# Loads of a streamed weight moved from the sync engine's list to the scalar engine's program

## What is computed

```
e    = 50 gathered table rows of 300 numbers for each batch row
h    = concat(attn_pool(e, w1..), attn_pool(e, w3..)) @ w5 + b5        # 300 wide
f7   = (h[:, iu] * h[:, ju] * g) @ w7 + b7      # all 44850 pairs i<j, w7 is 44850 x 300
out8 = concat(h @ w6 + b6, f7) @ w8 + b8
z    = einsum('bu,bku->bk', out8, label_embedding)   # 200 label rows of 300 for each batch row
y    = top MLP(concat(z, dense_ctx))
```

## Time and profile before

| | |
|---|---|
| runs | 2052.7, 2054.82, 2057.39 us; median 2054.82 |
| profiled execution | span 1864.9 us from the first to the last instruction; the page gives no device time of its own, and the median lies 189.9 us above the span |
| PE busy | 1703.9 us, 91% of the span |
| DVE busy | 1676.7 us, 90% |
| ACT busy | 1036.3 us, 56% |
| moved by DMA | 563.23 MB, mean 302 GB/s |
| SP's queue (q1) | 499.93 MB, 70.2% of the 16 engines' span |
| POOL's queue (q0) | 61.64 MB, 10.6% |

### The profile page before, as it was taken

The page is one execution under the profiler, slowest core; times in us unless marked ns, Lnnn a source line. Parts: engine busy times, 40 slices in busy tenths (PEclk is TensorE's granted clock), DMA queues, the critical chain, the costliest instruction groups (busy, mean ns, idle before and its releaser), DMA issues.

```text
span 1864.9 us, 26157 instructions
## 1 busy us (share of the span) xinstructions
PE 1703.9 (91%) x7132; PEld 1255.0 (67%) x7132; DVE 1676.7 (90%) x5836; ACT 1036.3 (56%) x3238; POOL 558.9 (30%) x413
## 2 busy tenths in 40 slices
PE   2788999999999999999999999999998999998841
PEld 1555667777777777777777677777776777775531
DVE  5898979989999889999999999899997888967785
ACT  3776684684466644466654675455753545454534
POOL 7774706828300134400078018500000000000053
PEclk8889999999999999999999999999999999999975
DMA  8378966757988689989768766998749999989985
GB/s 276 105 259 300 331 216 189 240 169 268 383 322 301 240 327 350 352 330 343 286 232 322 271 256 207 380 370 335 254 149 379 418 379 366 406 337 419 419 352 243
DMA packets 97949, 563.23 MB, mean 302 GB/s; under 512 B 16591, under 2 KB 16837, under 8 KB 72205
## 3 DMA queue, kind: packets, MB, share of 16 engines
q1 hardware_dynamic: 78525, 499.93, 70.2%
q0 software_dynamic: 19264, 61.64, 10.6%
q10 hardware_dynamic: 16, 0.00, 0.0%
HBM read 561.51 MB, written 0.00 MB: 301 GB/s over the span
## 4 chain that ended last, share of the span: by engine, by line
PE 54%; DVE 25%; DMA 11%; issue 4%; POOL 4%; ACT 3%; SPq 0%; DVEq 0%; ACTq 0%; POOLq 0%
PE acc L956 45%; DVE junk L580 11%; DVE qa L622 8%; DMA w_sb<-in_w 7%; DVE prod L734 6%; DMA lab<-in_labels 3%; POOL x L526 3%; PE coarse L807 2%; PE acc L872 1%; PE misc L879 1%; ACT heads L1067 1%; PE acc L941 1%; PE acc L854 1%; PE acc L857 1%; PE coarse L941 1%
## 5 line engine op out<-in xcount | busy, mean ns | idle before, releaser
L956 PE MATMUL acc<-w_sb,prod 128*128 128x300 f32 (+2 forms) x5680 | 1537.7, 421 | 52.9 <-DMA w_sb<-in_w 34.7
L956 PEld LDWEIGHTS acc<-w_sb,prod 128*128 128x128 f32 (+2 forms) x5680 | 1047.2, 192 | 402.8 <-DMA w_sb<-in_w 45.1
L1169 ACT ACTIVATE prod<-prod,g_all 128x256 f32<-128x256 f32 (+3 forms) x1625 | 690.7, 470 | 487.1 <-DVE prod L734 484.9
L526 POOL DMA_INDIRECT x<-in_tbl,ids_sb x376 | 485.8, 1292 | 672.5 <-DVE qa L622 565.2
L734 DVE TENSOR_TENSOR prod<-fine,coarse 128x1280 f32<-128x1280 f32 (+4 forms) x325 | 424.3, 1310 | 92.2 <-PE coarse L807 89.8
L580 DVE SCALAR_TENSOR_TENSOR junk<-lab,out 128x300 f32<-128x300 f32 x1056 | 424.6, 463 | 21.0 <-DMA lab<-in_labels 20.7
L580 DVE SCALAR_TENSOR_TENSOR junk<-x,score_u 128x300 f32<-128x300 f32 x752 | 303.6, 465 | 20.3 <-DMA x<-in_tbl,ids_sb 20.2
L622 DVE SCALAR_TENSOR_TENSOR qa<-x,ex,qa 128x300 f32<-128x300 f32 x628 | 282.6, 519 | 0.0
L557 POOL TENSOR_TENSOR x<-x,out 128x2400 f32<-128x2400 f32 x6 | 31.6, 5264 | 602.2 <-ACT out L1042 593.3
L1067 ACT ACTIVATE heads<-x 128x300 f32<-128x300 f32 x376 | 152.2, 405 | 25.8 <-DMA x<-in_tbl,ids_sb 24.8
L580 DVE SCALAR_TENSOR_TENSOR junk<-x,out 128x300 f32<-128x300 f32 x344 | 137.6, 463 | 0.0
(11 more groups left out here) (112 smaller groups left out, 628.0 us busy)
## 6 DMA issues: line engine op xcount, KB each, us to landing
w_sb<-in_w SPq DMA_DIRECT2D x325, 750.0 KB, 6.5
lab<-in_labels SPq DMA_DIRECT2D x140, 1200.0 KB, 7.8
x<-in_labels SPq DMA_DIRECT2D x60, 1200.0 KB, 8.7
x<-in_tbl,ids_sb POOLq DMA_INDIRECT x376, 5.5
prod<-in_v_i SPq DMA_DIRECT2D x1, 710.0 KB, 4.3
prod<-in_v_j SPq DMA_DIRECT2D x1, 710.0 KB, 7.3
w_sb<-in_w SPq DMA_DIRECT2D x1, 703.1 KB
top_sb<-in_top SPq DMA_DIRECT2D x1, 512.0 KB
```

Source lines behind the costliest of these rows:

```text
L526: pool.indirect_dma_start(out=row_of(t, n), out_offset=None, in_=tables[n], in_offset=bass.IndirectOffsetOnAxis(ap=ids_sb[:, t, n:n + 1], ...
L956: last = pe.matmul(acc[:, t % 3, 0:EMB], prod[0:rows, u % RING, m, t % 2 * P:(t % 2 + 1) * P], w7_sb[0:rows, u % W7_RING, m * EMB:(m + 1) ...
L1169: act.activation(chunk, chunk, ACT.Copy, scale=g_all[0:rows, pair:pair + 1]).then_inc(chunk_ready, 1)
```

## The change

SP issues only the first four loads of w7 and then the label slabs. The other 321 loads of w7 are issued by ACT, each right after it has scaled the last chunk of unit u, for unit u + 2. The condition on PE is the one of before (PE has finished unit n - 4, which is u - 2); new is that ACT must have finished scaling unit u, and that the transfers run on ACT's queue, which so far carried eight stores of 512 bytes.

```diff
             for kind, n in LOADS:
                 if kind == "w7":
-                    if n >= W7_RING:
-                        sp.wait_ge(unit_used, n - W7_RING + 1)
-                    sp.dma_start(w7_sb[:, n % W7_RING, :], w7[n % UNITS]).then_inc(w7_loaded[n % W7_RING], 16)
+                    if n < W7_RING:
+                        sp.dma_start(w7_sb[:, n, :], w7[n]).then_inc(w7_loaded[n], 16)
                     continue
...
+            def load_w7(n):
+
+                act.wait_ge(unit_used, n - W7_RING + 1)
+                act.dma_start(w7_sb[:, n % W7_RING, :], w7[n % UNITS]).then_inc(w7_loaded[n % W7_RING], 16)
+
...
                     if m == 1 and u + RING < TOTAL:
                         pick_window(u + RING)
+                    if m == FINE - 1 and W7_RING <= u + 2 < TOTAL:
+                        load_w7(u + 2)
```

## The result

The changed kernel took 2066.11 us (median of 7 runs, 2060.07 to 2069.23), the kernel before 2055.2 us beside it (7 runs, 2051.5 to 2058.04). The ratio is 1.0047, with a 95% interval of 1.0035 to 1.0059. That is a small loss of 9.7 us (7.2 to 12.1), against 6.6 us in the forecast.

What follows compares the result with a forecast made beforehand. Loads of w7 were late behind slabs in one queue, and DMA was the bound from 1660 us. Terms: -1.5 + 0 + 2.0 + 3.6 + 2.5 = 6.6 us slower, median 2054.8 to 2061.4 us, range 2046 to 2075.

Steps and rivals of the forecast that it cites:

- Sign and size: Whole kernel: slower by 6.6 us, the median going from 2054.8 to 2061.4 us; chance 0.42.
- Issue and wait on ACT, 0: ACT's program: 321 issues are covered by its waiting, and the new wait holds back nothing that could run; 0 us.
- A queue of its own: Loads of w7 beside a slab backlog: w7 gets 38% of 423 GB/s and lands in 6.9 us, including 2.1 us latency.
- The stall at 236 us: Load of unit 37: 4.1 us gained, 2.6 lost to three earlier slabs in the single-tile stage; net gain 1.5 us.
- The stalls at 1037 and 1205 us: Unit 180's load gains at most 3.9 us, offset by slabs: 0; at 1205 w7 passes a slab: 2.0 us lost.
- The stall at 1427 us: Before unit 248: PE's stall becomes a wait for the cross; two more loads pass the slab, 3.6 us lost.
- The end: From 1660 us, DMA-bound: later w7 issue and slabs not needed yet taking the rate lose 2.5 us.
- Later issue elsewhere: Loads also wait for the scaling two units ahead; unit 26's lead of 4.66 us just enough; 0, bounds 0 and 3.
- Waits of DVE for slabs above 23.8 us: Changed profile, whole span: DVE would wait for slabs more than 23.8 us in all.

Runs made afterwards that it cites:

- before again: Also called e1: the kernel before, unchanged, timed and profiled once more; 2048.78 us against 2047.65, ratio 1.0006, profiled span 2043.2 us.
- e5_after_two_slabs_first: The changed kernel with two label slabs moved in SP's list ahead of the burst of six slabs for `x`; ratio to the kernel before 0.9972.
- e10_end_act_slabs_held: The kernel before with ACT issuing the last 39 loads of w7, SP still waiting where it used to issue them; ratio 1.0044.
- e11_end_late_issue_sync: The kernel before, SP's loads of w7 for units 286 to 324 also waiting for the scaled chunks two units ahead; ratio 1.0034.

## Why the prediction was right, and where it was not

**Sign and size: right.** +6.6 us forecast, +9.7 (7.2 to 12.1) measured.

**Issue and wait on ACT, 0: right.** The wait alone gave 0.9999. The issues cost nothing either where nothing else changed: units 207 to 246 took 220.3 to 220.6 us and units 250 to 289 took 210.1 us, whether ACT issued their loads or SP.

**A queue of its own: the share was right, the latency too small.** The views give no landing times of loads on ACT's queue, but they count the packets of each queue. From 1600.2 to 1613.8 us after, when both streams had work waiting (packets, MB, share of the engines' time; q1 is SP's queue and q10 ACT's):

```profile
q1 hardware_dynamic: 425, 3.62, 62.9%
q10 hardware_dynamic: 390, 2.15, 38.1%
```

So w7 moved 2.15 of 5.77 MB, 37%, where I had assumed 38%. The times of its packets in the trace give the landings: the loads of units 247, 248 and 249 ended 8.4 to 8.7 us after their issue, not 6.9. Their bytes took 4.7 to 5.0 us, against the 4.8 of my sum; the first packet moved only 3.5 to 3.7 us after the issue, where I had put 2.1.

The slabs beside them say the same, by the landing of the first and of the fourth of the burst of six. After, issued at 1595.0 and 1596.3:

```profile
DMA to landing us min/median/max: 5.2/5.2/5.2
...
DMA to landing us min/median/max: 17.5/17.5/17.5
```

They landed 13.6 us apart, 4.5 us for each slab. All six of before again, issued from 1582.9 to 1585.6:

```profile
DMA to landing us min/median/max: 5.5/11.6/17.4
```

That is 14.6 us for five, 2.9 each. Slabs thus ran at 2.9 / 4.5 = 64% of the rate beside w7, where I had assumed 62%.

**The stall at 236 us, gain 1.5: the size may be luck.** The first slabs went out from 274 to 293 us, not at 320. Units 5 to 50 took 179.9 to 183.2 us in the six kernels with before's handling of them, mean 182.2, and 177.7 to 181.6, mean 180.1, in the five with after's: a gain of 2.1, less than single executions differ by. The stall that was to go wasn't there. In before again the load of unit 37 was as late as in the first profile (issued at 322.7, landed at 338.4 by its packets), but PE stood in unit 36 at that time, for nothing that the profile shows, and reached unit 37 at 345.6:

```profile
339.24 2.37 PE L956 MATMUL acc<-w_sb,prod 126*128 126x300 f32 x4 [6.10 <-issue]
```

The loss that was to come did: after, PE waited 3.7 us for w7 before units 22, 23 and 25, beside the slabs, against 2.6 in my sum. What gives the rest back isn't shown.

**The stalls at 1037 and 1205 us, 0 and a loss of 2.0: neither was there.** Both lie just behind places where the executions from e1 on had the erratic waits of DVE (units 176 and 205), which may have given the slabs time. Before again had no slab wait there either, and units 178 to 204 and 207 to 246 took the same in all. The step that failed is taking single stalls of one profiled execution for stalls of the timed runs. In their place stands one that I had not priced: DVE waited 1.64 us for a slab at 937.23, and units 118 to 175 took 0.3 to 3.7 us longer in every kernel in which ACT issues w7 there. (The gathers that I took to have a third of the rate near 1037 moved 2.17 of 8.08 MB, a quarter.)

**The stall at 1427 us, loss 3.6: right in mechanism.** DVE's wait was to be 13 to 14 us and was 13.62, 3.2 us more. PE lost 4.5 us from unit 246 to 250. `e5_after_two_slabs_first` shows the cause by taking it away.

**The end, loss 2.5: the term was mis-sized, and half of its reason was wrong.** It measured 5.8 us. I had given two reasons: loads issued later at the start of the stage, and slabs running ahead of need. `e10_end_act_slabs_held` takes the second away and loses as much; `e11_end_late_issue_sync` adds the first alone, with a longer delay, and loses 7 us. The lateness was bigger than I took it, because the load stands behind other work of ACT. And I had held that where DMA is the bound bytes are only handed on: the stretch ran at 403, 404 and 411 GB/s with the loads issued late (after and the two runs just named), with a DMA share of 1.00, and at 418 GB/s in before again. The bytes did not go to the other stream; fewer of them moved in the time. In `e11_end_late_issue_sync` the engines ran short of work; after, the slower slices have shares of 0.97 and more, and why less moved in them isn't shown.

**Later issue elsewhere, 0: right within the bound of 3 us, for a wrong reason in part.** I had the load go out when ACT has scaled the last chunk, which gave a lead of 4.66 us for unit 26, just enough. After, that lead was 8.5 us, since ACT issues ahead of its scaling (last section). Between units 5 and 36 the load went out a median of 7.7 us ahead of its use after and 8.9 in before again, and units 5 to 50 took no longer. A wait for the scaling itself, on SP's list, left 6.2 us there and cost 30 us in all.

**Waits of DVE for slabs above 23.8 us: wrong as a number,** 18.2, since the 23.8 belong to the other kind of execution; against 13.1 they rose.

## What to carry to other kernels

Splitting a queue changes two things at once: which bytes pass which, and what each issue waits behind in its new program. Price each at the place where the stream is tight, since both hide where it isn't. A stream that gets its own queue takes rate from the other, so the order within the other queue has to be set anew; here the move lost 0.5% alone and gained 0.3% with two slabs moved up. Where transfers are the bound, issue them as soon as their places fall free, from an engine that waits for nothing else.

## What the runs showed of the hardware

A profiled execution can lack waits that the timed ones have: 1864.9 us and 2043.2 us for the same kernel, whose timed runs lay between 2037 and 2064 us. The missing 180 us are idle time of PE, DVE and ACT, much of it marked as waiting for nothing that the profile shows, or for what it can't name. In before again near 1167 us DVE's steps, elsewhere 0.4 us apart, looked like this:

```profile
1168.03 0.47 DVE L580 SCALAR_TENSOR_TENSOR junk<-lab,out 128x300 f32<-128x300 f32 x1 [1.34 <-DVE junk L580]
1168.71 0.08 DVE L580 DVE_READ_ACCUMULATOR junk<-lab,out 128x1 f32 x1 [0.21 <-issue]
1169.43 0.47 DVE L580 SCALAR_TENSOR_TENSOR junk<-lab,out 128x300 f32<-128x300 f32 x1 [0.64 <-issue]
```

What causes them no run here was made to tell; that stays open.

ACT's queue issues a load before the activations that stand ahead of it in the program have ended. After, the load that follows the fifth scaling of unit 247 was issued at the same time as the first:

```profile
1606.29 0.51 ACT L1173 ACTIVATE prod<-prod,g_all 126x256 f32<-126x256 f32 x1 [2.13 <-DVE prod L733]
1606.31 0.33 ACTq L1000 DMA_DIRECT2D w_sb<-in_w  x1
```

The last of the five ended at 1608.70. So the issue is held by the waits ahead of it in the program, here the one for the cross, and not by the work.

Two queues with work waiting shared the bytes 37 to 63 (after, 1600.2 to 1613.8 us) where their rows have 6000 and 9600 bytes, which is 38 to 62. Loads issued beside the other queue's backlog moved their first packet after 3.5 to 3.7 us.
